# A four-layer gated cross-attention block: the routing plan's third part, V's projection and the first half's expert tiles at other positions

## What is computed

```python
x = x + tanh(g_xattn[0]) * L0_xattn(layernorm(x), ctx, ctx)       # 16 heads of 8, 512 keys
x = x + tanh(g_ffn[0])   * L0_ffn(layernorm(x))                   # top-1 of 8 experts, 128 -> 512 -> 128, relu
x = x + tanh(g_xattn[1]) * L1_xattn(layernorm(x), ctx)            # self-attention, cross-attention, FFN, each with a norm
x = x + tanh(g_ffn[1])   * L1_ffn(layernorm(x))                   # RoPE causal attention, then top-2 of 4 experts
```

## Time and profile before

| | us |
|---|---|
| median of 3 runs | 1185.59 |
| lowest, highest | 1184.12, 1190.38 |
| the profiled execution | 1189.5 |
| its span | 1187.5 |
| PE busy | 1049.7 (88%) |
| DVE, ACT, POOL busy | 790.0, 621.8, 367.8 |
| DMA, mean | 133 GB/s |

### The profile page before, as it was taken

How to read it: one execution, slowest core, us unless ns; L and a number is a source line. 1 busy time by engine, 2 the same in 40 slices (tenths; PEclk the granted TensorE clock), 3 DMA queues, 4 the chain that set the end, 5 groups by cost and what they waited for, 6 DMA issues and landing times. The chain is left out here.

```text
span 1187.5 us, 25293 instructions
## 1 busy us (share of the span) xinstructions
PE 1049.7 (88%) x8548; PEld 645.7 (54%) x8548; DVE 790.0 (67%) x1935; ACT 621.8 (52%) x1331; POOL 367.8 (31%) x982
## 2 busy tenths in 40 slices
PE   4999998799898698788799998897988889899998
PEld 1455554477454486445455554444555667656665
DVE  4788887533877524577688877869666777644443
ACT  1477764455564454456477775655644445543221
POOL 4333332221434422543433333413233435200000
PEclk9999998899987799788899999999998999999999
DMA  6655644464334663565665563543435355301000
GB/s 164 190 161 174 178 144 137 127 180 135 107 104 125 198 181 111 157 175 157 205 182 176 155 175 95 167 123 104 125 94 152 114 165 155 109 28 46 11 26 9
DMA packets 173173, 157.97 MB, mean 133 GB/s; under 512 B 13075, under 2 KB 146835, under 8 KB 172691
## 3 DMA queue, kind: packets, MB, share of 16 engines
q1 hardware_dynamic: 168854, 141.24, 40.4%
q0 software_dynamic: 4192, 15.12, 4.1%
HBM read 91.56 MB, written 66.85 MB: 133 GB/s over the span
## 5 line engine op out<-in xcount | busy, mean ns | idle before, releaser
L1110 ACT ACTIVATE prob<-ps 128x512 f32<-128x512 f32 (+1 forms) x768 | 400.2, 578 | 177.1 <-PE ps L1672 134.4
L1304 DVE TENSOR_REDUCE nmax<-ps 128x1 f32<-128x512 f32 x512 | 328.9, 685 | 82.6 <-PE ps L1637 81.3
L1672 PE MATMUL ps<-Qst,Kst 75*128 75x256 bf16 x1408 | 244.8, 284 | 15.8 <-DMA Qst<-mrow 8.7
L1637 PE MATMUL ps<-Kst,Qst 72*128 72x512 bf16 x512 | 198.7, 403 | 24.2 <-DVE nmax L1304 21.3
L1688 PE MATMUL av_ps<-prob,Vx 128*32 128x256 f32 (+1 forms) x3072 | 215.8, 398 | 0.6 <-ACT FB L1187 0.3
L1672 PEld LDWEIGHTS ps<-Qst,Kst 75*128 75x128 bf16 x1408 | 135.7, 101 | 86.5 <-ACT prob L1110 15.5
L1688 PEld LDWEIGHTS av_ps<-prob,Vx 128*32 128x32 f32 x3072 | 91.8, 114 | 66.4 <-issue 33.9
L1034 POOL TENSOR_TENSOR mparts<-nmax,zeros 128x8 bf16<-128x8 f32 x122 | 25.2, 206 | 306.1 <-issue 298.6
L1313 DVE TENSOR_REDUCE nmax<-ps 128x2 f32<-128x512 f32 x128 | 85.6, 687 | 47.9 <-PE ps L1651 47.2
L1637 PEld LDWEIGHTS ps<-Kst,Qst 72*128 72x128 bf16 x512 | 50.5, 99 | 106.6 <-DVE nmax L1304 53.2
L1114 ACT ACTIVATE OT<-av_ps 128x256 f32<-128x256 f32 x128 | 49.2, 385 | 108.7 <-PE av_ps L1688 108.1
(11 more groups left out here) (198 smaller groups left out, 1652.9 us busy)
## 6 DMA issues: line engine op xcount, KB each, us to landing
q_parts<-qp SPq DMA_DIRECT2D x96, 192.0 KB, 2.5
Qst<-q_parts SPq DMA_DIRECT2D x128, 144.0 KB
k_parts<-kp SPq DMA_DIRECT2D x46, 384.0 KB, 3.3
Kst<-k_parts SPq DMA_DIRECT2D x60, 288.0 KB
k_parts<-kp SPq DMA_DIRECT2D x48, 192.0 KB, 2.7
Kst<-k_parts SPq DMA_DIRECT2D x64, 144.0 KB
ctxT<-in_ctxT SPq DMA_DIRECT2D x16, 256.0 KB, 4.8
xs_rows<-in_blank SPq DMA_DIRECT2D x22, 128.0 KB, 4.1
```

Source lines behind the costliest of these rows:

```text
L1110: act.activation(prob[:, RING_AT[st] % RING, half * 512:half * 512 + w], bank(x)[:, 0:w], ACT.Exp).then_inc(drained(x), 1)
L1304: ve.tensor_reduce(nmax[:, g, u, h % GH:h % GH + 1], bank(st), AX.X, ALU.max, negate=True).then_inc(drained(st), 1)
L1637: last = pe.matmul(bank(st), Qst[0:ROWS, par, s, u * P:u * P + P], Ks[0:ROWS, par, s, :], start=True, stop=True)
L1672: last = pe.matmul(o, Ks[0:KROWS, par, h, t * P:t * P + P], Qst[0:KROWS, par, h, :], start=True, stop=not a.rope)
```

## The change

It does three things. The plan's third part goes from position 16 to 15, right behind the second. `v` goes from position 10 to 14 in the two bodies in which a plan is made (4 and 8): the projections of V for bodies 5 and 9. And the first half's `TILES_AT` goes from 24 to 27, which moves its x loads, tiles, the weight loads 4 to 10, and the chain `loadx` to `kstore` of bodies 8 and 9 by three positions. Scatters and weight loads 0 to 3 keep their positions, as does everything else of the second half.

```diff
@@ moe0_items
         put(n, 13, ("m0.rank", last, None))
         for k in range(3):
-            put(n, 14 + k, ("m0.plan", g, k))
+            put(n, (14, 15, 15)[k], ("m0.plan", g, k))
         put(n, 16, ("m0.wload", g, 0))
@@
+def plans(n):
+
+    return 0 < n <= B and n % HALF == 0
+
+
 def sends_near(n):
@@
-TILES_AT = (24, 26)
+TILES_AT = (27, 26)
@@ body
     if n + 1 < hi:
-        put(12 if a.rope else 10, ("v", n + 1, None))
+        put(14 if plans(n) else 12 if a.rope else 10, ("v", n + 1, None))
```

## The result

The kernel after is **slower**: 1197.03 us in the median of 17 runs (1189.16 to 1207.44) against 1186.72 of 17 runs of the kernel before on the same chip, ratio 1.0076, 95% interval 1.0051 to 1.0102, so 6 to 12 us. On another chip it came out again: 1193.74 against 1187.17, ratio 1.0063 (1.0025 to 1.0101). All ratios here leave out runs over 1.5% above the fastest of their kernel; from the second set of experiments on this drops more of the 23 to 35 runs of before than of the 6 or 12 of the others and puts a ratio up to 0.4% above that of the plain medians (t_c40: 1.0030 against 0.9996, chain3: 1.012 against 1.0078, p_again: 1.0061 against 1.0041). Forecast were 1178.5 and a range of 1173.5 to 1185.0. The profiled execution took 1199.77 us (span 1198.0, mean granted clock 0.935); that of before 1189.5 (1187.5, 0.95).

What follows compares the result with a forecast made beforehand. PE, 88% busy, was taken to bound the kernel, with x-tile stalls to win. Gains 5.76, 3.2, 0.4, 0.5, 1.6 less losses 1.4, 2.1, 0.9 made 7.1 us: 1178.5 against the median 1185.59, range 1173.5 to 1185.0.

Steps and rivals of the forecast that it cites:

- The stall of 5.76: First half, first transpose: PE's wait for the x tile goes, 5.76 us gained, with 0 to 1 left over.
- the half clock of 3.2 behind it: First tile stage behind the stall: the sequence transpose to AV runs at faster clock without the stall, 3.2 us gained.
- The x load issued near 222.5 and landing 3 to 4 us later: First half: issued three positions later with the weights nearly through, the x tile lands at 226, before PE needs it.
- the stall moves with the load: Rival, first half: the x load still takes 10.0 us and PE waits 4 us; 1184.8 us in all, chance 0.14.
- Vx late, 1.4 lost: First half's tiles: DVE's K split loses its cover, body 4's projection waits about 2.35 for Vx; 1.4 us lost, 0 to 2.4.
- The tail, 2.1 lost: Body 9's normalization: DVE meets it right behind the statistics and waits for POOL's reciprocal root; 2.1 us lost, 0 to 5.08.
- 0.9 for all new half clock: Behind the new waits for Vx and body 9's normalization: lowered clock, 0.9 us lost, taken between 0 and 3.2.
- the tail collides: Rival, behind the first half's tiles: row maxima and K come late, 16.0 us lost instead of 2.1; 1192.4, chance 0.07.
- Plan and V, first half, +0.5: Body 4 to position 1 of body 5: DVE's idle time shrinks; 0.5 us gained, between 2 lost and 2.2 gained.
- Plan and V, second half, +1.6: Second half: scatters start earlier without the wait for `ypos`, shortening PE's 8.48 us stall; 1.6 us gained, 0 to 2.2.
- earlier scatters give nothing: Rival, plan edit: second half's 1.6 becomes 0, first half loses 2 instead of gaining 0.5; 1182.6 us, chance 0.17.

Runs made afterwards that it cites:

- second set of experiments: Before and after rerun on another chip; after with the chain at its old place; before with plan and V edits. Against before: after 1.0063, others 1.0015 and 1.0039.
- t_c40: Before with the first half's tiles three positions later, chain of bodies 8 and 9 from position 40, body 9's statistics one position earlier; 1.0030 of before.
- chain3: Before with only the start of the first half's chain of bodies 8 and 9 moved from 38 to 41; 1199.11 against 1189.82 us, ratio 1.012.
- p_again: Before with only the plan's third part at position 15, run once more; 1.0061 of before (1.0025 to 1.0097).
- first set: Tiles, V and plan edits each alone on before, and after with an earlier chain; 1.0037, 0.9968, 0.9962 and 1.0034 of before, which took 1203.4 us.
- w_late: Before with the second half's three weight gathers of POOL put behind the attention's reciprocal root; 1181.86 against 1186.35 us, ratio 0.9985.
- tvw_c40: t_c40 with V at position 14 and the second half's three weight gathers behind the attention's root; median 1184.87 us, 1.0007 of before.
- p_only: Before with only the plan's third part at position 15; 0.9962 of before (0.9929 to 0.9995), where before took 1203.4 us.
- tail2: After with the first half's chain of bodies 8 and 9 only one position later than in before, not three; 1207.7 us against before's 1203.4, ratio 1.0034.
- t_xs9: Before with the first half's tiles and chain three positions later and body 9's statistics one position earlier; 1191.82 us, 1.0024 of before.

## Why the prediction was wrong, step by step

- **The stall of 5.76 and the half clock of 3.2 behind it.** The mechanism was right: no wait for the x tile, 0.87 of the clock, 8.9 us between the profiles, of which 1.95 only moved behind the mark. The size was read from one execution: over six the wait is 3.8 in the mean, and the whole stage, with Vx, gains 3.8 instead of 7.6.
- **The x load issued near 222.5 and landing 3 to 4 us later.** Right: issued at 224.85, landing in 3.2 us in the median in after (2.8 to 5.4 in the other kernels with the tiles at 27), and PE waits in none of them. The rival in which the stall moves with the load is out.
- **Vx late, 1.4 lost.** PE waited 2.12 at 228.98 (2.35 forecast). Lowered clock followed (0.66 from 228 to 232); it was not in the sum.
- **The tail, 2.1 lost, and 0.9 for all new half clock: the step that failed.** The place was named and the wait for the root came as described (DVE 2.58, PE 2.39). Missing was the wait of 1.70 fourteen microseconds earlier, where statistics of body 8 and the attention's own lie in one lump on DVE. The two new waits are 4.1 us, but smaller ones went, so idle time grew by only 1.0. What was missing above all is the price of the clock: 7.0 us of slower matmuls where 0.9 was put, and 5.9 in chain3. I bounded the clock by the 3.2 us behind the long stall. But the length of the slow phase does not follow the length of the pause: behind 2.39 us it lasted some 14 us, behind the 5.76 it cost 3.2.
- **The rival "the tail collides", given 0.07**, came nearest in time (1192.4) and had the right place. Its condition (body 8's K later than its first S) did not occur; it was DVE's queue that collided. So the time came near by luck: its sum has 16.0 us for the tail from other waits (with the 0.9 for half clock left in beside them), and the tail cost 9.0.
- **Plan and V, first half, +0.5.** Not resolved: 3.0 to 5.0 took 70.9 to 78.2 us outside the first set, in the mean 74.9 with both edits and 75.3 with neither.
- **Plan and V, second half, +1.6: not there.** The scatters began without their wait, but PE's wait for the x tile shrank by 0.2 us only, since SP's queue and the weight gathers stand between, and PE waited up to 2.9 us longer ahead of it for DVE. 8.0 to 10.0 is as long with the two edits as without (98.3 and 98.4). This is the rival "earlier scatters give nothing", which I priced at 0 in this half. That the weight gathers stand between is shown by w_late and tvw_c40; the part of SP's queue is read from one timeline and not tested. Whether the plan's edit costs something of its own, as p_again says and p_only denies, stays open.
- **The sum as it came out.** Against the means of the six profiles without the tile edit, and with the second layer put back where it was: 3.8 gained (tiles), 9.0 lost (tail, 45.0 against 34.0 less 1.95), together 5.2 us slower; forecast for the two were 7.6 gained and 2.6 lost. The medians lie 10.3 and 6.6 us apart. What makes up the other 1.4 to 5.1 us is not shown; the stretch from 10.0 to 16.0 alone varies by more than that in the same program.

## What to carry to other kernels

A step that moves takes its followers along: look at what stood behind the moved block at a fixed place (here body 9's normalization), because the distance to it shrinks by the whole shift. On a kernel like this one, with TensorE 88% busy, price a new wait of 2 us at what the clock may do behind it, and not at the wait: here 4.1 us of new waits came with 5.9 and 7.0 us of slower matmuls. Where stages are compared between two marks, count the matmuls in them first, since work can move across a mark. And take a second profile of the unchanged kernel before a sum of 7 us is built on a stall that one execution shows: this one was between 0.75 and 5.76 us.

## What was new about the hardware

- Behind a pause of PE of 1.84 us at 181 us the granted clock was low for about 4 us in before and for all 22 us of unbroken work in tail2; t_xs9, with the program of before up to there, was at 0.53 over the same 22 us, before at 0.81.
- A 128 KB load issued just behind three gathers of 592 KB landed 6.7 to 8.7 us after its issue in the second half (median of the first two loads, in the 13 profiles outside the first set that show it); without them ahead it landed in 3.1 and 3.2. The Trainium skill, DMA: Bandwidth & Descriptors, section Queues, rings and completion order, has each DMA engine alternate between its queues, which would let the load through. The measurement decides: here the load did not get through quickly, and in the first half, behind the same gathers, it took between 5.6 (p_again) and 10.0 us (before).
- One chip took 1203 us for what the others do in 1186 to 1190, with a stall of three engines at POOL's scatters of the first half and a longer body 8 at those of the second; its cause was not found.
